# Where the mask sums of an encoder half are written and read: two units move from SyncE's DMA queue to ScalarE's

## The chip, the cores and the metric

One core of one Trainium2 chip runs the whole program, in one launch. The metric is the device time of a launch in microseconds (us), as a median over runs of the same kernel.

## The reference

Input x is (2, 1024, 128) in float32, with 16 heads of 8. The reference is four layers with residuals, each behind a layer norm:

- softmax attention over 1024 keys and a projection,
- a feed-forward block with FP4 quantised weights and activations,
- an encoder of six layers, which holds most of the time: attention under a Sierpinski mask, then a GELU feed-forward of 512, with a layer norm after each,
- a feed-forward block with ReLU.

What the change concerns is the masked attention of the encoder:

```
scores = einsum(q, k) * scale
scores = scores * smask          # smask[i, j] = ((i & j) == 0)
a = softmax(scores)              # a masked key has score 0, not minus infinity
```

A masked key so still counts in the softmax, with exp(0 - max). The kernel computes only the allowed keys, and adds for the masked ones their number, and the sum of their values, times exp(-max). That factor needs the row maxima in another layout (queries on partitions) than the one in which they are found. The maxima are therefore written to HBM and read back: these are the "mask sums" of the title.

## The kernel before, in words

**Halves and units.** The encoder runs as 12 halves (6 layers by 2 batch rows), one behind the other. The scores of a half are worked in four units k = 0 to 3: k // 2 is the set of eight heads (whose K and Q stand in one "stack" of SBUF), k % 2 the half of the 1024 queries.

**Slots.** Every engine walks through the same 82 slots of a half (`pe_half`, `act_half`, `dve_half`), and in a slot it does what tables name, in this order: an A step, a B step, an AV bundle, then jobs.

- A step (66 in a half): TensorE scores into PSUM tile pA (L590), VectorE reduces them to maxima (L854). Behind the last A step of a unit VectorE runs `dve_max` (L802 on): it writes the maxima `emx` (L821) and three bf16 parts of them, `mt` (L838). pA has 3 banks.
- B step (82 in a half, lead 36 slots): TensorE scores again with the maximum taken off (pB, L605), ScalarE takes the exponential into PB (L722). pB has 2 banks, so TensorE's B step n waits for the exponential n - 2. B step n stands in slot 36 + n of its half; those from slot 82 on run beside the next half's A steps. The text calls the exponentials of a half number 0 to 81.
- AV bundle: TensorE multiplies PB with V (pO, L620).
- Jobs stand in the table `SPARSE_JOBS`, one list for each of TensorE, ScalarE and VectorE, as (slot, name). In `act` the names that matter are `ewk` and `erk` (write and read the mask sums of unit k), `emk` (exp(-max), L663), and around slots 44 to 62 `ht`, `qk`, `v`, `ft`, `hid` (evacuations for this and other halves). Within a slot ScalarE does the exponential first and then the jobs, in the order of the list.

All engines are in order. A job that waits holds up everything behind it on its engine.

**The mask sums of unit k.** `write_sums` (L950) waits until `dve_max` of the unit is through and writes emx to HBM with one DMA, 16 KB (L952). `load_sums` (L954) waits until that write has landed, and reads it back into emr with four DMAs of 4 KB (L958). `em` reads emr; it is due in slots 85 to 97, that is 3 to 15 of the next half. The buffer emx has two places, so `dve_max` of unit k + 2 waits for the landing of unit k's write.

**Before the change** units 0 and 1 go by SyncE: `move_max` (L939 on) issues the three DMAs QS<-mt (L944) and behind them the write and the four reads of the sums. Units 2 and 3 go by ScalarE, as jobs ew2 (slot 69), er2 (81), ew3 (83) and er3 (90).

**SyncE's order in a half** h (`sp_half`, L960): maxima of unit 3 of h - 1; QS of stack 1, first query half; maxima of unit 0; K of stack 1 (`load_k`, L930), and QS of stack 1, second query half (`load_q`, L921), both after the last B steps of h - 1; maxima of unit 1; `write_parts` of the first query half of h + 1 (L936, L937); in even halves the late weights; `write_parts` of the second; QS of stack 0 for h + 1 (L921); maxima of unit 2; K of stack 0 for h + 1 (L930) and QS again. TensorE waits for stack 1 in slot 48, at A step 33.

```
if a.sparse and k < UNITS // 2:
    write_sums(sp, a, half, k)
    load_sums(sp, a, half, k)
```

Of the kernel before, what the change touches and what calls it, by code (L numbers as in the profile page):

```python
# [41 lines left out]
UNITS = 4  # L42
# [146 lines left out]
class Attn:  # L189
# [96 lines left out]
    def ring(self, n):  # L286
# [42 lines left out]
def build(nc, io):  # L329
    ctx = ExitStack()  # L330
    with ctx:
# [607 lines left out]
        def move_max(sp, a, half, k):  # L939
            s, x = divmod(k, 2)  # L940
            half.wait(sp, a.mx, MXN * (k + 1), MXN * UNITS)
            half.wait(sp, a.m_loaded, 48 * k, 48 * UNITS)
            for i in range(NP):
                sp.dma_start(QS[R_A + i:R_A + i + 1, x, SH * s:SH * (s + 1), :].rearrange("p h t -> p (h t)"),  # L944
                             mt[:, x, i, :]).then_inc(a.m_loaded, 16)
            if a.sparse and k < UNITS // 2:
                write_sums(sp, a, half, k)
                load_sums(sp, a, half, k)

        def write_sums(eng, a, half, k):  # L950
            half.wait(eng, a.mx, MXN * (k + 1), MXN * UNITS)
            eng.dma_start(sce[half.b, k], emx[:, k % 2, :]).then_inc(a.e_written[k], 16)  # L952

        def load_sums(eng, a, half, k):  # L954
            half.wait(eng, a.e_written[k], 16, 16)
            src = sce[half.b, k].rearrange("(h q) (l w) -> l q h w", h=NQ, l=NQ)
            for l in range(NQ):
                eng.dma_start(emr[QT * l:QT * (l + 1), k, :, :], src[l]).then_inc(a.e_loaded[k], 16)  # L958

        def sp_half(sp, a, half, between=None):  # L960

            cur, prev, nxt = a.alive(half), a.alive(half + -1), a.alive(half + 1)
            if prev:
                move_max(sp, a, half + -1, 3)
            if cur and a.sparse:
                load_q(sp, a, half, 1, 0)
            if cur:
                move_max(sp, a, half, 0)
            if cur and not a.sparse:
                load_q(sp, a, half, 1, 0)  # L970
            if cur:
                load_k(sp, a, half, 1)
                load_q(sp, a, half, 1, 1)
                move_max(sp, a, half, 1)
            if nxt:
                write_parts(sp, a, half + 1, 0)
            if between is not None:
                between()
            if nxt:
                write_parts(sp, a, half + 1, 1)  # L980
                load_q(sp, a, half + 1, 0, 0)
            if cur:
                move_max(sp, a, half, 2)
            if nxt:
                load_k(sp, a, half + 1, 0)
                load_q(sp, a, half + 1, 0, 1)
# [564 lines left out]
```

## Time and profile before

| | |
|---|---|
| median of 3 runs | 2010.36 us (2009.47 to 2013.61) |
| profiled execution | 2019.47 us |
| its span | 2017.7 us, so 1.8 us lie around it |
| granted TensorE clock, mean | 0.911 of full speed |
| TensorE matmuls busy | 1660.8 us, 82% of the span |
| VectorE busy | 1397.0 us, 69% |
| ScalarE busy | 1187.9 us, 59% |
| GpSimd busy | 254.7 us, 13% |

The encoder fills the span from about 690 to 1940 us, some 104 us for each half but the last. The profile's rows name the line of the kernel, the tiles as out<-in, the count, and in brackets the idle time of the engine before an instruction with what ended it. "issue" is an engine that waits for nothing that the profile shows. SPq and ACTq are the sequencers of SyncE and ScalarE, which issue the DMAs.

### The profile page before, as it was taken

The numbers are of one execution on the slowest core, as the hardware profiler recorded it, in microseconds if no ns is written. First come the engines' busy times: TensorE is split into PE (matmuls) and PEld (weight loads), VectorE is DVE, ScalarE is ACT, GpSimd is POOL, SyncE is SP. The second block draws the span as 40 slices with busy tenths as digits, with TensorE's granted clock in tenths as the row PEclk, the third lists the DMA queues.
The fourth block names the chain that finished last, engine by engine and source line by source line (L and its number), as shares of the span: only waits on it lengthen the run. The fifth ranks groups of instructions, "written<-read, shape, count | busy, mean of one in ns | idle before, by whom it ended". The sixth has DMA issues, their size and how long they took to land.

```text
span 2017.7 us, 66915 instructions
## 1 busy us (share of the span) xinstructions
PE 1660.8 (82%) x28905; PEld 921.2 (46%) x28905; DVE 1397.0 (69%) x3285; ACT 1187.9 (59%) x2117; POOL 254.7 (13%) x229
## 2 busy tenths in 40 slices
PE   2889999997564578888888888888889898989677
PEld 1133333332343145555555555555555555555445
DVE  7788888883475665858686867676767675767824
ACT  2057777776312165767666767676766666766542
POOL 1000000000000301212121212120202020202111
PEclk8579999998776589999999999999999899999889
DMA  6022102000002543333333433343243333342001
GB/s 151 16 49 77 37 3 49 2 2 2 14 0 64 117 110 70 88 71 106 85 90 67 114 66 95 66 110 80 71 95 87 96 79 83 70 120 52 5 2 32
DMA packets 152205, 130.83 MB, mean 65 GB/s; under 512 B 65014, under 2 KB 147382, under 8 KB 149894
## 3 DMA queue, kind: packets, MB, share of 16 engines
q1 hardware_dynamic: 134629, 125.75, 25.7%
q8 instruction: 228, 3.74, 0.8%
q10 hardware_dynamic: 17280, 0.79, 0.6%
q14 instruction: 68, 0.55, 0.1%
HBM read 79.25 MB, written 45.88 MB: 62 GB/s over the span
## 4 chain that ended last, share of the span: by engine, by line
PE 54%; DVE 21%; ACT 11%; issue 7%; DMA 6%; POOL 1%; SPq 1%; ACTq 0%; POOLq 0%; DVEq 0%
PE pB L605 12%; PE pO L620 12%; PE pA L590 9%; ACT PB L722 5%; DVE mx L854 5%; PE pG L561 5%; PE pG L571 5%; DMA emr<-sce 3%; PE pG L511 2%; DMA QS<-scq 2%; DVE bst L427 2%; ACT VD L682 2%; ACT HT L637 2%; PE pG L538 1%; PE pG L525 1%
## 5 line engine op out<-in xcount | busy, mean ns | idle before, releaser
L722 ACT ACTIVATE PB<-pB 128x512 f32<-128x512 f32 (+1 forms) x1496 | 836.7, 593 | 478.2 <-PE pB L605 456.8
L854 DVE TENSOR_REDUCE mx<-pA 128x1 f32<-128x512 f32 (+3 forms) x1000 | 636.7, 670 | 146.5 <-PE pA L590 145.5
L605 PE MATMUL pB<-QS,KS 85*32 85x256 bf16 (+3 forms) x11264 | 600.1, 285 | 73.2 <-ACT PB L722 44.5
L590 PE MATMUL pA<-KS,QS 82*32 82x256 bf16 (+2 forms) x8384 | 545.3, 313 | 95.7 <-DMA QS<-scq 48.7
L620 PE MATMUL pO<-PB,VD 128*32 128x128 f32 (+3 forms) x5632 | 459.2, 400 | 5.0 <-issue 3.1
L605 PEld LDWEIGHTS pB<-QS,KS 85*32 85x32 bf16 x11264 | 262.7, 97 | 363.7 <-ACT PB L722 250.9
L590 PEld LDWEIGHTS pA<-KS,QS 82*32 82x32 bf16 x8384 | 203.3, 98 | 319.5 <-DVE mx L854 108.3
L854 DVE TENSOR_REDUCE mxb<-pA 128x1 f32<-128x512 f32 x304 | 207.2, 681 | 9.4 <-PE pA L590 9.4
L450 POOL TENSOR_TENSOR rstd<-vareps,mhalf 128x4 f32<-128x4 f32 x68 | 69.2, 1018 | 1115.7 <-DVE vareps L436 1114.7
L620 PEld LDWEIGHTS pO<-PB,VD 128*32 128x32 f32 x5632 | 160.9, 112 | 32.4 <-issue 5.9
L561 PE MATMUL pG<-HT,wL 128*128 128x512 f32 x192 | 100.4, 650 | 27.4 <-ACT HT L637 25.1
L758 DVE TENSOR_TENSOR ON<-pG,em 128x288 f32<-128x288 f32 x48 | 20.7, 453 | 122.5 <-ACT em L663 122.4
L462 PE MATMUL pG<-ident,N 128*128 128x128 f32 x320 | 55.7, 301 | 48.0 <-DMA QS<-in_qzero 20.1
L571 PE MATMUL pG<-wL,FF 128*128 128x128 f32 x768 | 91.8, 278 | 3.5 <-ACT FF L658 3.5
L571 PEld LDWEIGHTS pG<-wL,FF 128*128 128x128 f32 x768 | 87.6, 192 | 9.4 <-ACT FF L658 9.4
L898 POOL TENSOR_TENSOR VU<-VN 128x512 f32<-128x512 f32 x12 | 16.3, 1360 | 554.3 <-PE pG L530 554.3
L658 ACT ACTIVATE FF<-pG,cL 128x512 f32<-128x512 f32 x96 | 66.0, 687 | 25.5 <-PE pG L561 23.7
L767 DVE TENSOR_TENSOR ON<-ON,pG 128x288 f32<-128x288 f32 x48 | 21.7, 452 | 85.2 <-PE pG L538 84.4
L511 PE MATMUL pG<-HT,wE 128*128 128x512 f32 x112 | 71.1, 726 | 10.3 <-ACT HT L637 9.9
L561 PEld LDWEIGHTS pG<-HT,wL 128*128 128x128 f32 x192 | 34.8, 201 | 79.2 <-issue 47.7
L462 PEld LDWEIGHTS pG<-ident,N 128*128 128x128 f32 x320 | 36.9, 149 | 71.7 <-issue 21.4
L443 DVE TENSOR_SCALAR N<-N,mv,rstd 128x128 f32<-128x128 f32 x208 | 57.9, 342 | 10.7 <-POOL rstd L450 10.4
(160 smaller groups left out, 1517.8 us busy)
## 6 DMA issues: line engine op xcount, KB each, us to landing
scq<-PQ SPq DMA_DIRECT2D x84, 384.0 KB, 3.5
QS<-scq SPq DMA_DIRECT2D x56, 576.0 KB
KS<-sck SPq DMA_DIRECT2D x84, 384.0 KB
sck<-PK SPq DMA_DIRECT2D x28, 384.0 KB, 5.6
wL<-in_wL SPq DMA_DIRECT2D x6, 576.0 KB, 4.9
QS<-mt SPq DMA_DIRECT2D x168, 8.0 KB, 2.1
rE<-in_rE SPq DMA_DIRECT2D x7, 256.0 KB, 12.2
emr<-sce SPq DMA_DIRECT2D x96, 4.0 KB, 1.7
```

What stands on the lines that cost most here:

```text
L443: ins = v.tensor_scalar(dst[:, t, :], src[:, t, :], mv[:, t, 0:1], rstd[:, t:t + 1], ALU.subtract, ALU.mult)
L450: g.tensor_tensor(rstd[:, a], vareps[:, a], mhalf[:, a], ALU.pow).then_inc(ln.rs, 1)
L462: ins = pe.transpose(pG[:, bank, i * P:(i + 1) * P], src[:, TC * c + i, :], ident[:, :])
L511: pe.matmul(pG[:, bank, :], wE[:, n[1], :], HT[:, c * CH:(c + 1) * CH], start=True, stop=True)\
L561: pe.matmul(pG[:, bank, :], wL[:, D + n[1] * P:D + (n[1] + 1) * P], HT[:, c * CH:(c + 1) * CH], start=True, stop=True).then_inc(F1.filled, 1)
L571: ins = pe.matmul(pG[:, bank, i * P:(i + 1) * P], FF[:, x, k, i * P:(i + 1) * P], wL[:, D + HID + k * D:D + HID + (k + 1) * D], start=(k = ...
L590: ins = pe.matmul(pA[QT * hd:QT * (hd + 1), a.a_bank(half, n), at:at + width], QS[0:R_A, r // NR, head, r % NR * QT:(r % NR + 1) * QT], ro ...
L605: ins = pe.matmul(pB[32 * i:32 * (i + 1), a.b_bank(h, v), at:at + width], KS[0:R_B, head, k0:k0 + 32], allowed(QS[0:R_B, x, head, :], 3, k ...
L620: ins = pe.matmul(allowed(pO[32 * j:32 * j + 32, k % OBANKS, :], 3, kt & 7 if a.sparse else 0), VD[:, col:col + 32], PB[:, a.ring(bank)[0] ...
L658: act.activation(FF[:, x, m, :], pG[:, a.bank[name], :], ACT.Gelu, bias=cL[:, 2 + m:3 + m])\
L722: act.activation(PB[:, pos_, 0:st.cols], pB[:, a.b_bank(h, v), 0:st.cols], ACT.Exp).then_inc(a.b_exped, 1)
L854: v.tensor_reduce(dst[:, gs[0]:gs[-1] + 1, tl[0]:tl[-1] + 1:step], pA[:, a.a_bank(half, n), 0:len(gs) * len(tl) * st.width] .rearrange("p ...
```

## The change

The two lines of code that gave units 0 and 1 to SyncE go, and four jobs enter ScalarE's table: ew0 in slot 44, er0 in 50, ew1 in 58, er1 in 62. The functions that they call are the ones that ew2 to er3 already call. The number of DMAs and their bytes stay as they are.

```diff
-    "act": [(83, "ew3"), (85, "em0"), (88, "em1"), (88, "em2"), (90, "er3"), (97, "em3"), (106, "oev2"),
+    "act": [(44, "ew0"), (50, "er0"), (58, "ew1"), (62, "er1"),
+            (83, "ew3"), (85, "em0"), (88, "em1"), (88, "em2"), (90, "er3"), (97, "em3"), (106, "oev2"),
...
             for i in range(NP):
                 sp.dma_start(QS[R_A + i:R_A + i + 1, x, SH * s:SH * (s + 1), :].rearrange("p h t -> p (h t)"),
                              mt[:, x, i, :]).then_inc(a.m_loaded, 16)
-            if a.sparse and k < UNITS // 2:
-                write_sums(sp, a, half, k)
-                load_sums(sp, a, half, k)
```

## Rows read from the trace of the kernel before

**Rows 1.** The page, part 1: busy us, share of the span, instructions
```profile
PE 1660.8 (82%) x28905; PEld 921.2 (46%) x28905; DVE 1397.0 (69%) x3285; ACT 1187.9 (59%) x2117; POOL 254.7 (13%) x229
```

**Rows 2.** Busy time by window, the encoder: window, its length, busy (count), clock, DMA
```profile
690.00:1940.00 1250.00, 1079.29 (x22949) 688.45 (x22950) 868.09 (x2255) 829.24 (x1457) 211.67 (x190) 0.96 0.34 81
```

**Rows 3.** The waits of the encoder, 690 to 1940 us: total us, times, longest
```profile
ACT PB L722 <- PE pB L605: 351.4, 307, 36.8
...
PE pB L605 <- ACT PB L722: 34.3, 62, 1.5
...
PE pB L605 <- issue: 16.8, 11, 4.0
...
PE pA L590 <- issue: 9.8, 14, 1.6
...
PE pA L590 <- DMA QS<-scq: 3.7, 1, 3.7
```

**Rows 4.** The tile sce: issuing time in ns, min/median/max, first and last start
```profile
L958 ACTq DMA_DIRECT2D emr<-sce x96: 309/453/880, 753.5 to 1903.4; - x96
L952 SPq DMA_DIRECT2D sce<-emx x24: 584/594/1522, 692.6 to 1864.0; - x24
L952 ACTq DMA_DIRECT2D sce<-emx x24: 344/346/532, 742.4 to 1897.0; - x24
```

**Rows 5.** Timeline of SyncE's queue, first half: start, us, what
```profile
692.55 1.31 SPq L952 DMA_DIRECT2D sce<-emx  x1
694.95 1.73 SPq L958 DMA_DIRECT2D emr<-sce  x4
696.78 1.15 SPq L930 DMA_DIRECT2D KS<-sck  x3
```

**Rows 6.** Timeline of TensorE, first half, at A step 33
```profile
710.30 0.62 PE L590 MATMUL pA<-KS,QS 82*32 82x512 bf16 x4 [3.74 <-DMA QS<-scq]
```

**Rows 7.** Timeline of SyncE's queue, the sixth half
```profile
1203.85 0.59 SPq L952 DMA_DIRECT2D sce<-emx  x1
...
1208.50 1.14 SPq L930 DMA_DIRECT2D KS<-sck  x3
...
1255.20 2.38 SPq L936 DMA_DIRECT2D scq<-PQ  x3
```

**Rows 8.** Timeline of ScalarE, the sixth half, around er2 and ew3
```profile
1272.26 1.71 ACT L722 ACTIVATE PB<-pB 128x512 f32<-128x512 f32 x3
1273.38 1.76 ACTq L958 DMA_DIRECT2D emr<-sce  x4
1275.24 0.60 ACT L722 ACTIVATE PB<-pB 128x512 f32<-128x512 f32 x1 [1.27 <-PE pB L605]
1275.35 0.39 ACTq L952 DMA_DIRECT2D sce<-emx  x1
1275.74 1.21 ACT L722 ACTIVATE PB<-pB 128x512 f32<-128x512 f32 x2
```

**Rows 9.** Timeline of ScalarE, the sixth half, at slots 44 and 50
```profile
1225.57 1.08 ACT L722 ACTIVATE PB<-pB 128x512 f32<-128x512 f32 x2 [1.27 <-PE pB L605]
...
1242.06 0.60 ACT L722 ACTIVATE PB<-pB 128x512 f32<-128x512 f32 x1 [2.58 <-PE pB L605]
```

**Rows 10.** Timeline of ScalarE, the sixth half, slots 56 to 68
```profile
1253.15 3.04 ACT L722 ACTIVATE PB<-pB 128x512 f32<-128x512 f32 x5
1256.51 2.68 ACT L722 ACTIVATE PB<-pB 128x512 f32<-128x512 f32 x4 [0.32 <-PE pB L605]
1259.09 0.59 ACT L675 ACTIVATE FF<-pO 128x512 f32<-128x512 f32 x1
1259.56 2.20 ACT L722 ACTIVATE PB<-pB 128x512 f32<-128x512 f32 x4
```

**Rows 11.** The same stretch on TensorE and on VectorE, by timeline
```profile
1260.22 0.40 PE L605 MATMUL pB<-QS,KS 85*32 85x256 bf16 x8 [0.33 <-ACT PB L722]
...
1255.09 6.40 DVE L854 TENSOR_REDUCE mx<-pA 128x1 f32<-128x512 f32 x11
```

**Rows 12.** TensorE's timeline, seventh and eighth half, slots 65 to 68
```profile
1365.10 0.61 PE L605 MATMUL pB<-QS,KS 85*32 85x256 bf16 x6 [1.49 <-issue]
...
1468.69 0.40 PE L605 MATMUL pB<-QS,KS 85*32 85x512 bf16 x3 [1.62 <-issue]
```

**Rows 13.** The writes issued at 1263.4 and at 1275.4 by ScalarE: us to landing
```profile
DMA to landing us min/median/max: 3.2/3.2/3.2
...
DMA to landing us min/median/max: 8.7/8.7/8.7
```

## The prediction

> **What bounds the kernel now.** I read the page's busy times first, then the busy time by window, the waits, and the timelines of the places where something is taken out or put in. TensorE's matmuls fill 82% of the span, ScalarE 59% [rows 1]. In the encoder, 690 to 1940 us, TensorE is busy for 1079 of 1250 us, 86%, VectorE for 868 and ScalarE for 829, at a granted clock of 0.96 [rows 2]. The waits say the same: ScalarE stands idle 351 us for TensorE's B scores, TensorE 34 us for ScalarE's exponentials [rows 3]. So TensorE is the bound, but on average only. Both of the other engines are in a loop with it of two or three banks, and where it runs through cheap slots they are level with it: in slots 58 to 68 of the sixth half VectorE does 11 reductions back to back (6.40 us, 0.58 each) and the exponentials follow each other at 0.55 to 0.67 us [rows 10, 11]. A delay of ScalarE costs nothing in one slot and all of itself in another. SyncE is the bound nowhere: in the whole encoder TensorE waits once for a stack, 3.7 us [rows 3], and that is in the first half [rows 6].
>
> **What is taken off SyncE.** For each of 24 units one write (0.59 us to issue [rows 4]), the wait for its landing, and four reads (1.73 us [rows 5]). From the write's issue to the free queue that is 4.2 us in the first half (692.55 to 696.78 [rows 5]) and 4.65 us in the sixth (1203.85 to 1208.50 [rows 7]). Queued behind unit 0's are K and Q of stack 1; behind unit 1's, write_parts for the next half. In the first half no older B steps hold the stack back: the K load starts 4.2 us earlier, the stack lands as much earlier, and TensorE's 3.74 us of idle time at A step 33 [rows 6] goes. I take -3.7 us, once; its bounds are 0 (the loads go slower, or something else is late next there) and -3.74. In the other eleven halves no such wait exists [rows 3], so an earlier load gains nothing: 0. What hides it is the distance from the load to slot 48. The QS<-mt transfers stand ahead of the removed ones and don't move. VectorE's dve_max of units 2 and 3 waits for the writes of units 0 and 1; these now go out in slots 44 and 58 and are needed in 68 and 80, 24 and 22 slots later, so 0.
>
> **What is put on ScalarE.** Four jobs in each of 12 halves, five DMAs a unit. Their prices stand in the trace, since ew2 to er3 are the same calls.
>
> A write (ew0, ew1): 0.35 us of issuing [rows 4]. At 1275.35 one was issued under the exponential that began at 1275.24, and the next began at 1275.74, without a gap [rows 8]. The sequencer runs ahead by one instruction, so a write is hidden under the exponential before it, here in slots 44 and 58 too (in 44, two of them stand back to back at 1225.57 [rows 9]). I take 0; if that cover were gone it would be 0.35 us each, 24 x 0.35 = 8 us. Their wait, for dve_max, is long over: unit 0's maxima left at 1203.85 [rows 7], slot 44 is at 1225.6.
>
> A read (er0, er1): four DMAs, 1.76 us, begun with the exponential before them at 1273.38, and the next exponential came at 1275.24, 1.27 us after that one's end [rows 8]. So a read leaves ScalarE idle for 1.27 us.
>
> er0 stands in slot 50, behind the exponential before 1242.06. There ScalarE is idle for 2.58 us, because TensorE works on the FFN's output jobs [rows 9]. 1.27 fits under 2.58: 0. Uncovered it would be up to 1.27 x 12 = 15 us. Its write is out for some 14 us by then.
>
> er1 stands in slot 62, behind exponential 26. In the sixth half that one begins at 1256.51 + 0.67 = 1257.2; the next would begin 1.86 us later, at 1259.1, where it now begins at 1257.85. ScalarE is 1.2 us late. TensorE's B step 29 needs exponential 27, which then ends at 1259.7; B step 31 runs at 1260.22 and even now waits 0.33 us for ScalarE [rows 11], so TensorE hasn't any slack left, and comes out 1.0 us late. VectorE has no idle time in its 11 reductions either, and only some 0.2 us between a score and its reduction: 0.8 us late. Queued behind er1 are the exponentials 27 to 33, oev0, and the write of unit 2, which waits for VectorE. I take 0.9 us as what one half passes on if nothing takes it up.
>
> What can take it up is a stop of TensorE of another origin, whose end doesn't move. Behind this place the trace shows some: 1.49 us at 1365.10 and 1.62 us at 1468.69, ended by "issue" [rows 12], and 0.17 only in the sixth half. In all, TensorE's score groups have 16.8 + 9.8 us of such stops in the encoder [rows 3]. If the stop's end stays, er1 is free in that half; if it moves along, er1 costs its 0.9. Bounds: 12 x 0 and 12 x 0.9 = 10.8 us. I take two thirds, 0.6 us a half, 7.2 us, since nothing in the trace shows those stops to be tied to the time and not to TensorE's own progress.
>
> On the chip's instruction fetch, the Trainium skill (Runtime: NRT & Kernel Launch, "Instruction fetch mechanics") says that crossing a block of instructions is mostly hidden. By that rule there is little to take the delay up, and the sum would be 10.8 - 3.7 = +7.1 us. The stops of 1.5 us [rows 12] don't fit that rule, if they are fetches, which the trace doesn't tell.
>
> **The sum.** -3.7 + 0 + 0 + 0 + 7.2 = +3.5 us. On the profiled execution, span 2017.7 and 1.8 around it, that is 2023.0; the executions without a profile lie lower, so on their median of 2010.36 it is 2013.9. A measurement of this kernel tells about 0.2%, 4 us, from no change; the forecast lies just inside.
>
> **Rivals.**
>
> Slower, all passed on: nothing takes up er1, and its issue is dearer, since it falls into the write_parts of the second query half (1255.20 [rows 7]); single issues have taken up to 0.88 us [rows 4]. 12 x (0.9 to 1.6) - 3.7 = +7 to +15.5 us: 2017 to 2026. For it speaks that all three engines are level there; against it, the stops of rows 12. It decides the sign from 0.65 us a half on (0.65 x 12 - 3.7 = +4.1).
>
> Slower, a new wait: er1 waits for ew1's landing. The two are 4 slots apart, 1254.4 to 1257.2, 2.8 us. ScalarE's writes have taken 3.2 us and, issued behind a bulk of loads, 8.7 us [rows 13]. With 8.7 every half loses 5.9 us on top: 12 x 5.9 = +71, 2084 us. The point from which it costs is a landing of 2.8 us. Against it: ew1 goes out at about 1254.4, 0.8 us before SyncE's bulk at 1255.20 [rows 7], both following from the same evacuation in every half, and unhindered landings are shorter than that (unit 0's reads began 2.4 us after their write's issue [rows 5]).
>
> Faster: ScalarE's delay is taken up in nearly all halves, the first half's 3.7 us come in full, and the queue that is 4 us less held up brings its bulk out of the way of one or two of TensorE's stops of 1.5 us. -3.7 - 0 to 3 = -4 to -7 us: 2003 to 2006. For it speaks that such stops stand close behind er1 in two of the three halves opened; against it, that the transfers which move (K of stack 1, the first write_parts) aren't beside those stops. On what a second queue can give, the Trainium skill (DMA: Bandwidth & Descriptors, "Issuing engines are not separate DMA queues") says that issuing from several engines only saves sequencer time. By that rule no landing gets quicker, and the gain is the first half's alone.
>
> No effect: the first half's gain is eaten by a later wait there, and er1 is taken up: 2010 us.
>
> **How the numbers follow.** Forecast (er1 partly taken up, +3.5, own range -2 to +7): 0.55, of it 0.35 within 0.2% and 0.20 above. All passed on: 0.17, slower. New wait: 0.03, slower. Faster: 0.20, of it 0.17 below by over 0.2%. No effect: 0.05. Together 0.17 faster, 0.35 + 0.03 + 0.05 = 0.43 same, 0.20 + 0.17 + 0.03 = 0.40 slower. The range takes in the faster case's larger part and the whole of the costlier er1, 2004 to 2024; only the new wait and the tails are left out.
>
> **What would show it.** SyncE's queue without L952 and L958, K of stack 1 issued at about 692.5 in the first half, and TensorE's 3.74 us there gone. On ScalarE, ew0 and ew1 without a gap behind them, er0 inside an idle time that stays near 2.6 us, er1 with a gap of 1.2 to 1.3 us in each half, and behind it TensorE's B step 29 waiting some 0.9 us for L722. The times from half to half 0 to 0.9 us longer. I am wrong if the gap at er1 is much above 1.3 us (then look for the landing of ew1's write), if er0 or ew0 show one of their own, or if the end of the encoder moves though these gaps are as said.

## The result, and the profile after

Changed 2028.52 us (median of 5, 2024.18 to 2032.36), before 2009.47 us (5 runs, 2006.92 to 2013.61). The ratio is 1.0089, interval 1.0067 to 1.0111: slower by 18 us, 13 to 22. The forecast was 2013.9 with a range up to 2024. The profiled execution took 2028.52, span 2026.7. That of before lay 10 us above its own median, so the two spans (2026.7 and 2017.7) show only half of the difference.

The busy times don't move: the page of the changed kernel has every engine within 5 us of [rows 1], and 0.8 MB have gone from SyncE's queue (q1) to ScalarE's (q10).

```profile
PE 1658.0 (82%) x28905; PEld 917.0 (45%) x28905; DVE 1398.9 (69%) x3285; ACT 1188.2 (59%) x2117; POOL 254.9 (13%) x229
...
q1 hardware_dynamic: 117349, 124.96, 24.9%
q10 hardware_dynamic: 34560, 1.59, 1.1%
```

The time is in the waits. These are the waits of the changed kernel's encoder, 690 to 1950 us (one line was added above, so L723 is L722 of before, L606 is L605, L591 is L590); they answer to [rows 3].

```profile
ACT PB L723 <- PE pB L606: 332.4, 304, 36.5
...
PE pB L606 <- ACT PB L723: 62.4, 77, 3.0
...
ACT PB L723 <- issue: 31.5, 11, 3.5
...
PE pB L606 <- issue: 12.7, 7, 3.9
...
PE pA L591 <- issue: 3.2, 7, 1.0
```

Two rows tell the story. ScalarE now stands idle before an exponential for 31.5 us in 11 times, up to 3.5, waiting for nothing but its own sequencer. Ten of the 11 are er1; behind er1 of the second and ninth half the idle time (1.90 and 2.08 us) is put down to TensorE instead. Over all 12 halves er1 leaves 2.8 us of idle time in the mean, and its four issues last 3.2. And TensorE waits for ScalarE's exponentials for 62.4 us where it was 34.3, 28 us more, the longest 3.0 instead of 1.5. Its stops of other origin ("issue") fell from 26.6 to 15.9 us.

In the fifth half, ScalarE's timeline, then SyncE's, then TensorE's, around slot 62:

```profile
1149.18 0.34 ACTq L950 DMA_DIRECT2D sce<-emx  x1
1149.84 1.26 ACT L723 ACTIVATE PB<-pB 128x512 f32<-128x512 f32 x2
1151.42 1.33 ACT L723 ACTIVATE PB<-pB 128x512 f32<-128x512 f32 x2 [0.32 <-PE pB L606]
1152.16 3.83 ACTq L956 DMA_DIRECT2D emr<-sce  x4
1156.09 1.08 ACT L723 ACTIVATE PB<-pB 128x512 f32<-128x512 f32 x2 [3.34 <-issue]
```
```profile
1150.11 1.61 SPq L937 DMA_DIRECT2D scq<-PQ  x3
1151.77 1.21 SPq L938 DMA_DIRECT2D sck<-PK  x1
1153.08 0.95 SPq L922 DMA_DIRECT2D QS<-scq  x1
```
```profile
1153.45 0.43 PE L591 MATMUL pA<-KS,QS 82*32 82x256 bf16 x8
1156.74 0.62 PE L606 MATMUL pB<-QS,KS 85*32 85x512 bf16 x4 [2.86 <-ACT PB L723]
```

The write (ew1, 1149.18) leaves no gap. The read (er1) begins where I had put it, with exponential 26, but its four issues take 3.83 us, not 1.76 as er2's do [rows 8]. They stand in a burst of five issues of SyncE, beside the last two of it. TensorE stands 2.86 us. The issuing times of the tile sce show the tail that [rows 4] had not:

```profile
L956 ACTq DMA_DIRECT2D emr<-sce x192: 309/454/2265, 708.2 to 1912.4; - x192
L950 ACTq DMA_DIRECT2D sce<-emx x48: 344/344/467, 700.7 to 1906.0; - x48
```

The median of a read's issue is still 0.45 us, the longest 2.27 instead of 0.88.

Slot 50, same half, ScalarE's timeline: er0 is stretched too, but between its last evacuation and exponential 15, whose idle time stays at the 2.58 us of [rows 9].

```profile
1132.36 0.31 ACTq L956 DMA_DIRECT2D emr<-sce  x1
1132.50 1.28 ACT L723 ACT_TABLE_LOAD   x1
1132.71 2.00 ACTq L956 DMA_DIRECT2D emr<-sce  x2
1133.79 0.60 ACT L723 ACTIVATE PB<-pB 128x512 f32<-128x512 f32 x1
1134.73 1.28 ACTq L956 DMA_DIRECT2D emr<-sce  x1
1136.97 0.60 ACT L723 ACTIVATE PB<-pB 128x512 f32<-128x512 f32 x1 [2.58 <-PE pB L606]
```

In the first half the K load goes out at 691.18, and TensorE's idle time at A step 33 is 1.37 us for 3.74 [rows 6]:

```profile
691.18 2.04 SPq L931 DMA_DIRECT2D KS<-sck  x3
```
```profile
705.09 0.40 PE L591 MATMUL pA<-KS,QS 82*32 82x512 bf16 x4 [1.37 <-DMA QS<-scq]
```

The two encoders don't start at the same time, so I count from the first exponential (695.43 before, 693.95 after). A step 33 then comes 14.87 us behind it before and 11.14 after: 3.7 us earlier. Exponential 14 comes 20.7 us behind it before and 14.5 after: 6.2 us earlier. The 2.4 us between the two are TensorE's clock. From A step 33 to exponential 14 it does the same 46 matmuls, before and then after (window, its length, busy time by engine, clock, DMA):

```profile
710.30:716.08 5.78, 5.73 (x46) 1.94 (x46) 1.33 (x3) 2.35 (x4) 0.00 (x0) 0.50 0.05 3
```
```profile
705.09:708.44 3.35, 3.10 (x46) 1.30 (x46) 2.11 (x4) 2.24 (x5) 0.00 (x0) 1.00 0.03 2
```

Behind the wait of 3.74 us the granted clock was 0.50, the lower of TensorE's two levels (1.2 GHz); behind the one of 1.37 us it was 1.00 (2.4 GHz).

### The profile page after: what moved, and what is told of

Read it like the earlier page. It is cut to its first block, busy times and chain, and to the rows that moved or that the text cites. A ratio compares the mean times of both kernels' runs of the same rounds, so it can differ in the third digit from the quotient of the medians.

```text
span 2026.7 us, 66915 instructions
## 1 busy us (share of the span) xinstructions
PE 1658.0 (82%) x28905; PEld 917.0 (45%) x28905; DVE 1398.9 (69%) x3285; ACT 1188.2 (59%) x2117; POOL 254.9 (13%) x229
## 3 DMA queue, kind: packets, MB, share of 16 engines
q8 instruction: 228, 3.74, 0.8%
## 4 chain that ended last, share of the span: by engine, by line
PE 54%; DVE 18%; ACT 12%; DMA 7%; issue 6%; ACTq 2%; SPq 1%; POOL 1%; DVEq 0%; POOLq 0%
PE pB L606 12%; PE pO L621 11%; PE pA L591 9%; ACT PB L723 6%; PE pG L562 5%; PE pG L572 5%; DVE mx L855 4%; DMA emr<-sce 4%; PE pG L512 2%; ACTq L956 2%; DMA QS<-scq 2%; DVE bst L428 2%; ACT VD L683 2%; ACT HT L638 2%; PE pG L539 1%
## 5 line engine op out<-in xcount | busy, mean ns | idle before, releaser
L723 ACT ACTIVATE PB<-pB 128x512 f32<-128x512 f32 (+1 forms) x1496 | 836.4, 593 | 489.8 <-PE pB L606 437.2
L606 PE MATMUL pB<-QS,KS 85*32 85x256 bf16 (+3 forms) x11264 | 599.6, 286 | 96.5 <-ACT PB L723 72.5
L591 PE MATMUL pA<-KS,QS 82*32 82x256 bf16 (+2 forms) x8384 | 545.2, 315 | 85.1 <-DMA QS<-scq 46.1
L606 PEld LDWEIGHTS pB<-QS,KS 85*32 85x32 bf16 x11264 | 261.5, 98 | 386.4 <-ACT PB L723 275.8
L591 PEld LDWEIGHTS pA<-KS,QS 82*32 82x32 bf16 x8384 | 203.1, 99 | 312.4 <-DVE mx L855 106.4
L444 DVE TENSOR_SCALAR N<-N,mv,rstd 128x128 f32<-128x128 f32 x208 | 57.9, 341 | 10.7 <-POOL rstd L451 10.5
```

Source lines behind the costliest of these rows:

```text
L444: ins = v.tensor_scalar(dst[:, t, :], src[:, t, :], mv[:, t, 0:1], rstd[:, t:t + 1], ALU.subtract, ALU.mult)
L591: ins = pe.matmul(pA[QT * hd:QT * (hd + 1), a.a_bank(half, n), at:at + width], QS[0:R_A, r // NR, head, r % NR * QT:(r % NR + 1) * QT], ro ...
L606: ins = pe.matmul(pB[32 * i:32 * (i + 1), a.b_bank(h, v), at:at + width], KS[0:R_B, head, k0:k0 + 32], allowed(QS[0:R_B, x, head, :], 3, k ...
L723: act.activation(PB[:, pos_, 0:st.cols], pB[:, a.b_bank(h, v), 0:st.cols], ACT.Exp).then_inc(a.b_exped, 1)
```

## The experiments

Each is compared with the kernel before in the same session. The diffs are against the changed kernel.

| run | median us | ratio to before, interval |
|---|---|---|
| changed kernel | 2028.52 | 1.0089 (1.0067 to 1.0111) |
| u1_act: only unit 1 on ScalarE | 2037.39 | 1.0146 (1.0121 to 1.0170) |
| er1_slot70 | 2016.40 | 1.0037 (1.0015 to 1.0059) |
| parts_later | 2014.94 | 1.0051 (1.0025 to 1.0078) |
| parts_later_2 | 2019.58 | 1.0052 (1.0019 to 1.0084) |
| before_again | 2008.94 | 0.9990 (0.9973 to 1.0008) |
| er1_spread | 2004.50 | 0.9978 (0.9957 to 0.9999) |
| u0_act: only unit 0 on ScalarE | 2004.17 | 0.9972 (0.9953 to 0.9991) |
| er1_slot51 | 2002.00 | 0.9973 (0.9954 to 0.9993) |
| no_er1 | 2001.52 | 0.9973 (0.9952 to 0.9995) |
| er2_early | 1985.12 | 0.9880 (0.9849 to 0.9912) |
| er3_spread | 1979.92 | 0.9847 (0.9816 to 0.9879) |

**Which unit: u0_act and u1_act.** Each undoes the change for the other unit.

```diff
# u0_act (u1_act has k == 0 and keeps ew1, er1)
-    "act": [(44, "ew0"), (50, "er0"), (58, "ew1"), (62, "er1"),
+    "act": [(44, "ew0"), (50, "er0"),
...
+            if a.sparse and k == 1:
+                write_sums(sp, a, half, k)
+                load_sums(sp, a, half, k)
```

Expected for u0_act:

> Unit 0's sums on ScalarE (ew0, er0), unit 1's back on SyncE. My theory (the loss is er1 in slot 62, whose four issues are stretched by SyncE's write_parts there): the loss goes altogether, exponential 27 follows 26 within 0.7 us again, and the first half keeps its shortening, so 2003 to 2009 us, 0 to 0.3% below the kernel before. Rival (unit 0's jobs, or the earlier start of SyncE's transfers, cost the time): still 2015 to 2025.

Expected for u1_act:

> Unit 1's sums on ScalarE (ew1, er1), unit 0's back on SyncE. My theory: nearly the whole loss stays, and the first half's gain is gone: 2027 to 2036 us, with 2.5 to 4 us from exponential 26 to 27 in each half. Rival (unit 0): within 5 us of the kernel before.

Measured 0.9972 and 1.0146. Unit 0 alone makes the kernel 0.28% faster than before; unit 1 alone makes all of the loss, and more than the changed kernel's, since the first half's gain is missing. The waits of u0_act's encoder:

```profile
PE pB L606 <- ACT PB L723: 36.2, 63, 1.5
...
ACT PB L723 <- issue: 3.6, 2, 2.3
```

TensorE's wait for ScalarE is back at 36 us, where [rows 3] has 34.3, and er1's 31.5 us are gone. The rival, that unit 0's jobs or the shifted transfers cost the time, falls.

**Which job: no_er1.** The four reads of unit 1 are left out, and em1 reads unit 0's sums.

```diff
-    "act": [(44, "ew0"), (50, "er0"), (58, "ew1"), (62, "er1"),
+    "act": [(44, "ew0"), (50, "er0"), (58, "ew1"),
...
-                hw(act, a.e_loaded[x], 64, 64)
+                if x != 1:
+                    hw(act, a.e_loaded[x], 64, 64)
...
-                    emr[:, x, :, :].rearrange("p h (r g) -> p h r g", g=2), ACT.Exp, scale=-1.0)\
+                    emr[:, 0 if x == 1 else x, :, :].rearrange("p h (r g) -> p h r g", g=2), ACT.Exp, scale=-1.0)\
```

> The changed kernel without the four reads of unit 1's sums (em1 reads unit 0's); ew1 stays in slot 58. If er1 is the whole loss: as with unit 0 alone on ScalarE, 2001 to 2007 us. If ew1 costs something too, the rest shows here: 2 us or more above that run.

Measured 0.9973, the same as unit 0 alone: ew1 costs nothing that the intervals of 4 us to either side show, er1 is the whole loss. Against the changed kernel that is 1.0089 - 0.9973 = 1.16%, 23 us, or 1.9 us in each of 12 halves. The traces say the same at the place itself: exponentials 26 to 34 take 9.7 us in the mean of the halves in the changed kernel, 7.2 in no_er1 and 7.4 to 7.5 in both traces of before.

**Place or neighbour: parts_later.** SyncE holds back its second write_parts until exponential 28 is done, behind er1.

```diff
+            if cur and nxt and a.sparse:
+                half.wait(sp, a.b_exped, 29, a.nb)
             if nxt:
                 write_parts(sp, a, half + 1, 1)
```

> The changed kernel, but SyncE issues the write_parts of the second query half only after exponential 28, so behind er1. Theory that SyncE's issues at the same time stretch er1: its four issues take 1.76 us again, 26 to 27 is 1.9 us, and er1 costs the 0.9 us a half that I had forecast: 2010 to 2018 us. Rival that er1's place alone costs it (any read in slot 62): issues still above 2.5 us, time as the changed kernel's, 2024 to 2032.

Measured 1.0051, half way: 0.4% goes (8 us by the ratios, 14 by the medians), and 0.8% over u0_act, 16 us, stays. The interval still touches the changed kernel's, so by the times alone the 0.4% is likely; the traces bear it out, with 8.9 us from exponential 26 to 34 here, 8.3 in the second trace below, and 9.7 in the changed kernel. So the neighbour is part of the price, and the rest of it stays without the neighbour. But the issues weren't at 1.76 us in all halves: they last 2.5 us in the mean. The same kernel, run for a second trace:

> A second trace of the kernel whose write_parts come after er1, since the first one's execution lay 16 us above its median. Expected: 2009 to 2020 us, er1's issues about 2.5 us in the mean as in the first trace, those without an instruction fetch beside them at 1.76 us.

1.0052 again, its median of 2019.6 at the upper edge of what was expected; er1's issues last 2.3 us in the mean. Its trace holds the answer in two halves that follow each other: ScalarE's timeline in the sixth, then in the seventh.

```profile
1257.13 1.76 ACTq L956 DMA_DIRECT2D emr<-sce  x4
1258.99 1.08 ACT L723 ACTIVATE PB<-pB 128x512 f32<-128x512 f32 x2 [1.27 <-PE pO L621]
```
```profile
1359.21 2.77 ACTq L956 DMA_DIRECT2D emr<-sce  x4
1362.08 1.09 ACT L723 ACTIVATE PB<-pB 128x512 f32<-128x512 f32 x2 [2.28 <-issue]
```

SyncE issues nothing in either stretch. In the sixth, er1 takes 1.76 us and leaves 1.27 us of idle time, to the hundredth what I had forecast. In the seventh it takes 1.0 us longer. The DMA queues of the two stretches, 1257.1 to 1259 and 1359.2 to 1362.2 us, have ScalarE's own q10 in common and differ in one line, which the second has alone: packets, MB, share of 16 engines.

```profile
q8 instruction: 1, 0.02, 2.4%
```

One block of instructions was on its way while er1 was issued. That isn't one pair of halves only. I sorted all 396 groups of four reads that ScalarE issues in the encoder, in ten of the traces (the kernel before twice, the changed one, u0_act, u1_act, no_er1, parts_later twice, er1_slot70, er1_slot51), by what else went on while they were issued:

| SyncE meanwhile | block in q8 | groups | four issues, mean us (range) |
|---|---|---|---|
| issues nothing | no | 115 | 1.77 (1.76 to 1.90) |
| issues nothing | yes | 45 | 2.23 (1.76 to 3.21) |
| issues write_parts | no | 45 | 2.69 (1.76 to 3.52) |
| issues write_parts | yes | 48 | 3.29 (2.18 to 4.54) |
| issues maxima (QS<-mt) alone | no | 76 | 1.82 (1.76 to 2.43) |

The other 67 groups stand beside other issues of SyncE, or beside maxima with a block. With neither neighbour nor block no group was ever stretched; each of the two goes with a stretching of its own. No run moved a block, so that it is the cause, and not what comes with it, isn't shown. In parts_later and its second trace SyncE issues nothing beside any er1, and a block is on its way during 22 of the 24, which fits a mean above 1.76. In the four halves of the second trace whose er1 is unstretched (2, 6, 9, 10), exponentials 26 to 34 take 7.5 us against 6.7 in the same halves of no_er1: 0.9 us, the forecast. The Trainium skill (Runtime: NRT & Kernel Launch, "Instruction fetch mechanics") has engines refill their instructions in 16 KiB blocks, mostly hidden; the packet here is the 0.02 MB of q8, and the issues beside it weren't as short as the others.

**The same by place: er1_slot70.** er1 behind ew2, outside write_parts.

```diff
-    "act": [(44, "ew0"), (50, "er0"), (58, "ew1"), (62, "er1"),
+    "act": [(44, "ew0"), (50, "er0"), (58, "ew1"), (70, "er1"),
```

> The changed kernel with er1 in slot 70, behind ew2, outside SyncE's write_parts. If only the issues' stretching by SyncE made the loss: issues of 1.8 us, 2008 to 2016 us, like the run with write_parts later. If the place in a stretch where ScalarE is waited for is enough, the same; 2003 us would say that ScalarE has slack there.

Measured 1.0037, 2016.4 us, the upper end; 0.65% over u0_act, 13 us, 1.1 a half. The issues were not all of 1.8 us, since SyncE has the maxima of unit 2 to send in this place. ScalarE, then SyncE, in the sixth half:

```profile
1259.66 3.30 ACTq L956 DMA_DIRECT2D emr<-sce  x4
1263.07 1.09 ACT L723 ACTIVATE PB<-pB 128x512 f32<-128x512 f32 x2 [2.83 <-PE pO L621]
```
```profile
1259.16 2.68 SPq L945 DMA_DIRECT2D QS<-mt  x3
```

A block of instructions is on its way here too, from 1259.96 to 1261.40, and it is what goes with SyncE's 2.68 us for three issues: in 11 of the 12 groups of maxima of this trace that stand beside ScalarE's reads without a block they take 1.76 to 1.77 us, as they do alone, and 2.12 in one. ScalarE's er1 takes 3.05 us in the mean in the six halves with a block and 2.07 in the six without, where SyncE's maxima are its only neighbour.

**A covered place: er1_slot51.** ew1 behind the FFN's evacuations of slot 49, er1 in slot 51.

```diff
-    "act": [(44, "ew0"), (50, "er0"), (58, "ew1"), (62, "er1"),
+    "act": [(44, "ew0"), (50, "er0"), (51, "er1"),
...
-          (131, "hid10"), (131, "hid11"), (131, "hid12"), (131, "hid13"), (-29, "v0"), (-28, "ht1"),
+          (131, "hid10"), (131, "hid11"), (131, "hid12"), (131, "hid13"), (49, "ew1"), (-29, "v0"), (-28, "ht1"),
```

> The changed kernel with ew1 at the end of slot 49's jobs and er1 in slot 51, behind exponential 15, where ScalarE waits for TensorE's jobs (2.08 us from one exponential to the next). If the place is what costs: 2003 to 2010 us; since er0's issues may run into er1's wait for ew1's landing there, some of the 2 us may be exceeded, up to 1 us a half, 2015 us. Rival (a read on ScalarE costs 2 us wherever it is): 2025 us.

Measured 0.9973, 2002.0 us: the whole loss gone, with all four units on ScalarE. ScalarE's timeline in the sixth half: the read stands in idle time that is there anyway. (In the first, fourth, eighth and eleventh half a block is on its way during er1, and the idle time behind it is 1.9 to 3.6 us instead of 1.47; the loss of that, if any, is within the interval.)

```profile
1231.96 0.60 ACT L723 ACTIVATE PB<-pB 128x512 f32<-128x512 f32 x1 [2.58 <-PE pB L606]
1231.97 1.78 ACTq L956 DMA_DIRECT2D emr<-sce  x4
1234.04 1.09 ACT L723 ACTIVATE PB<-pB 128x512 f32<-128x512 f32 x2 [1.47 <-PE pB L606]
```

**A covered form: er1_spread.** The four reads in slots 62 to 65, one behind each exponential (`load_sums` gets the number of the read).

```diff
-    "act": [(44, "ew0"), (50, "er0"), (58, "ew1"), (62, "er1"),
+    "act": [(44, "ew0"), (50, "er0"), (58, "ew1"), (62, "ra1"), (63, "rb1"), (64, "rc1"), (65, "rd1"),
```

> The changed kernel with the four reads of er1 in four slots, 62 to 65, one behind each exponential. If what costs is that four issues in a row are longer than the one exponential that covers them: each of 0.45 us is covered, and 2003 to 2010 us come out; issues stretched to over 0.6 us still cost, up to half of the loss, 2014 us. Rival (the reads load the DMA engines or hold up instruction fetch, wherever they are issued): 2020 to 2030 us.

Measured 0.9978, 2004.5 us. The same DMAs, begun at the same place beside the same write_parts, cost nothing above the interval (4 us to either side) when each has an exponential above it. So the loss isn't the reads' load on the DMA engines; it is the sequencer's time in one piece.

**The kernel before, again: before_again.**

> The kernel before, unchanged, for a second trace: the profiled execution of before lay 10 us above the median. Expected: the same time within 0.2%, and halves whose slots 0 to 70 take the same time as in the first trace; what differs from trace to trace should be the stretch from exponential 34 on.

0.9990, within the 0.2% expected. Its span is 2008.6 us, and its first exponential of the encoder begins at 691.35, 4 us earlier than in the first trace (695.4), so not all of the 9 us between the two traces lie where I had put them.

**Two versions beyond both.** er2 stands in the half's end in four issues in a row, too, and its landing under the K load of the next half is what em2 waits for. er2_early takes er1_slot51 and puts er2's reads into slots 73 to 76; er3_spread puts er3's into 90 to 93 as well.

```diff
# er2_early, against er1_slot51
-           (-27, "qk10"), (-27, "qk11"), (64, "oev0"), (69, "ew2"), (-10, "v1"), (77, "oev1"), (81, "er2")],
+           (-27, "qk10"), (-27, "qk11"), (64, "oev0"), (69, "ew2"), (-10, "v1"), (77, "oev1"),
+            (73, "ra2"), (74, "rb2"), (75, "rc2"), (76, "rd2")],
# er3_spread, against er2_early
-            (83, "ew3"), (85, "em0"), (88, "em1"), (88, "em2"), (90, "er3"), (97, "em3"), (106, "oev2"),
+            (83, "ew3"), (85, "em0"), (88, "em1"), (88, "em2"), (90, "ra3"), (91, "rb3"), (92, "rc3"), (93, "rd3"), (97, "em3"), (106, "oev2"),
```

> The kernel with er1 in slot 51, and the four reads of er2 moved from slot 81 to slots 73 to 76, one each, ahead of SyncE's K load for the next half. If a read of four in a row costs 1.27 us wherever ScalarE is waited for, and er2's landing of 9 to 11 us under that load is what em2 and VectorE wait for: 0.5 to 2 us less in each half than with er1 in slot 51, 1980 to 1997 us. Rival (the half's end is bound by ew3's landing and TensorE's own stops): within 0.2% of 2002 us.

> As er2_early, with the four reads of er3 in slots 90 to 93, too. er3 waits for ew3's landing in any case, and its issues then stand in a stretch in which ScalarE is 0.25 us behind TensorE at most: up to 1.2 us less in each half, 0 to 14 us below er2_early. Rival: no change, since em3 in slot 97 comes to wait for the last read.

Measured 0.9880 and 0.9847: 1985.1 and 1979.9 us, 24 and 31 us below the kernel before. The tile em tells why, in its waits in er1_slot51, the kernel that er2_early was made from, and then in er2_early. The DMA line is what ScalarE waits for ahead of em, the two last lines are who waits for em:

```profile
  DMA emr<-sce: 22.0, 8
...
  DVE ON L759: 120.9, 23
  PE pG L539: 30.3, 8
```
```profile
  DVE ON L762: 100.4, 23
  PE pG L540: 11.9, 1
```

ScalarE's wait for the landing of the reads is gone, and TensorE waits 18 us less, about what the kernel gained (0.9973 to 0.9880, 19 us). The slowest of er2's four reads lands 7.9 to 9.4 us after its issue in 11 halves of er1_slot51; in er2_early it lands after 4.8 to 6.9 us in ten of them and 10.7 in one, and it is issued five slots or more earlier. How much is the landing and how much the spreading wasn't separated. The intervals of the two versions overlap, so that the second is better than the first is likely, not shown.

## Why the prediction was wrong, point by point

**What bounds the kernel**: right. SyncE's relief is seen in the first half, and ScalarE's delay is passed to TensorE where the three are level.

**What is taken off SyncE, -3.7 us once**: right in sign, place and mechanism, and too small for a term left out. A step 33 comes 3.7 us earlier behind the first exponential, as forecast, though 1.37 us of its idle time remain. What the sum doesn't have is the clock behind the wait. In both traces of before and in u1_act, whose waits are 3.7 to 4.4 us, TensorE was granted 0.50 to 0.64 of full speed from A step 33 to exponential 14, and 1.00 in the changed kernel. From the first exponential to number 26 the first half takes 39.8, 39.8 and 38.9 us in those three, and 32.7 to 36.3 us, 33.9 in the mean, in the ten traces with unit 0 off SyncE: 5.6 us. The times agree: u0_act, no_er1 and er1_slot51 stand at 0.28% below the kernel before, 5.5 us, with intervals from 1 to 9.6 us. That the wait brings the lower clock fits all these traces; no run held the wait and changed only the clock.

**ew0, ew1 and er0 at 0**: right. no_er1 and u0_act are equal, and er0's idle time is 2.58 us as before, even where its issues last from 1132.36 to 1136.01.

**er1: the step that failed is its price.** "1.76 us, begun with the exponential before them": place and start were right. In a quiet half the sum was right too: 1.27 us of idle time, and 0.9 us passed on, is what parts_later_2 shows. But I took er2's duration for er1's, from a place beside two of SyncE's maxima, the neighbour that stretched the issues least, and er1 stands beside write_parts in 10 of its 12 halves and beside a block of instructions in 9. Its issues last 3.2 us in the mean and leave 2.8 us of idle time, not 1.27. TensorE's wait grew by 28.1 us against before and by 25.0 against no_er1, the kernel that lacks er1 alone, which is 2.3 or 2.1 us a half, not 0.9. Where the sum had 7.2 us for er1, the runs show 23. My bounds for it, 0 to 0.9 us, held only what could be taken off; dearer issues stood in a rival, and there at 0.9 to 1.6, from the longest issue of 0.88 us. That row was of reads beside maxima; a bound for the crowded place would have come from SyncE's reads in the same view, of which the longest took 1.68 us:

```profile
L958 SPq DMA_DIRECT2D emr<-sce x96: 303/432/1681, 695.0 to 1867.0; - x96
```

**What takes it up, a third**: not borne out. TensorE's stops of other origin fell from 26.6 us in the first trace of before (21.0 in the second) to 15.9. But they are 16.1 us in u0_act, 15.5 in no_er1 and 12.5 in er1_slot51 too, where er1 delays nothing, so the fall isn't er1's delay being taken up. Against no_er1 the wait for ScalarE grew by 25.0 us, and the time by 23: nearly all of it was passed on.

**The sum with measured terms**: -5.5 for the first half and +25 us for er1 is +19.5 us, against a measured 18 (13 to 22).

**The rivals.** "All passed on, and its issue is dearer" named both steps, the price and that nothing is taken up, and was sized at +15.5 at most. The new wait for ew1's landing does occur, in three halves of 12, and is 0.2 to 0.4 us: in the third half er1 begins 3.18 us after ew1, 0.2 after its exponential. No block is on its way there, so its 3.03 us go with write_parts alone.

```profile
937.71 0.34 ACTq L950 DMA_DIRECT2D sce<-emx  x1
...
939.95 1.33 ACT L723 ACTIVATE PB<-pB 128x512 f32<-128x512 f32 x2 [0.32 <-PE pB L606]
940.89 3.03 ACTq L956 DMA_DIRECT2D emr<-sce  x4
944.02 0.60 ACT L723 ACTIVATE PB<-pB 128x512 f32<-128x512 f32 x1 [2.74 <-issue]
```

The faster rival's sign holds for unit 0 alone.

## What to carry to other kernels

In this kernel DMA issues on ScalarE were free one at a time, each under the exponential before it. Four in a row have only one exponential above them, and left 1.3 us of idle time in the quiet case and 2.8 in the mean beside another queue's burst. Look for where that engine already waits longer than the issues take, or spread them one to an instruction; and take their duration from a place as crowded as the one they go to, with the same neighbours. A read whose landing somebody waits for belongs ahead of the next bulk load, not behind it. When a wait of TensorE goes, look at its granted clock behind the wait as well as at the wait.

## What the runs showed of the hardware that I had not expected

The time in which a sequencer issues a DMA isn't its own. Four reads of 4 KB took ScalarE 1.77 us in the mean, and never over 1.90, where SyncE issued nothing and no block of instructions was on its way; 2.69 beside write_parts, 2.23 with a block, 3.29 with both. The kind of neighbour matters: beside SyncE's maxima they took 1.82. With a block on its way SyncE's three maxima took up to 2.9 us instead of 1.77 in er1_slot70; beside ScalarE's reads and without a block they stayed at 1.77 in 11 cases of 12. The Trainium skill (DMA: Bandwidth & Descriptors, "Issuing engines are not separate DMA queues") says that issuing from several engines saves only the sequencer's time. No run here tests the "only". What the runs add is that two sequencers issuing at the same time can lose part of that time, too. By what the neighbour or the block holds the issues up wasn't tried.
